# Computing the first key pair by eight plain products, and splitting the context on VectorE

## The reference, cut to what matters

```python
x = _rmsnorm(hidden_states, ln_weight)
h_q = (x @ w_q.T).reshape(b, lq, H, DH)
h_k = (key_value_states @ w_k.T).reshape(b, lk, H, DH)   # key_value_states is ctx_4096
h_v = (key_value_states @ w_v.T).reshape(b, lk, H, DH)
score = jnp.einsum('bqhd,bkhd->bhqk', h_q, h_k) + position_bias[None]
```

## Time and profile before

| | us |
|---|---|
| Median of 3 runs | 1058.89 |
| Lowest and highest run | 1058.1, 1059.1 |
| The profiled execution, its own time | 1058.91 |
| Its span, first to last instruction | 1056.8 |
| TensorE busy in the span | 1014.0 (96%) |
| VectorE, ScalarE, GpSimd busy | 730.2, 505.9, 481.7 |

### The profile page before, as it was taken

How to read it: one execution, slowest core, us unless ns; L and a number is a source line. 1 busy time by engine, 2 the same in 40 slices (tenths; PEclk the granted TensorE clock), 3 DMA queues, 4 the chain that set the end, 5 groups by cost and what they waited for, 6 DMA issues and landing times.

```text
span 1056.8 us, 17513 instructions
## 1 busy us (share of the span) xinstructions
PE 1014.0 (96%) x5850; PEld 887.6 (84%) x5850; DVE 730.2 (69%) x1316; ACT 505.9 (48%) x1226; POOL 481.7 (46%) x413
## 2 busy tenths in 40 slices
PE   8599999989999999999999999999999999799995
PEld 8488788878999998989898989898999998578784
DVE  6968776647777777676767676767777777663615
ACT  6545444535455455454454554545545455344251
POOL 2645776436345354363553544535535443443204
PEclk9799999999999999999999999999999999899998
DMA  7433444431221221202112212021121230300011
GB/s 259 139 117 123 150 167 162 173 123 52 91 65 52 79 74 42 92 25 92 62 55 79 66 50 91 26 92 62 54 80 41 75 112 21 110 20 1 0 41 40
DMA packets 39140, 86.07 MB, mean 81 GB/s; under 512 B 5184, under 2 KB 9280, under 8 KB 39104
## 3 DMA queue, kind: packets, MB, share of 16 engines
q1 hardware_dynamic: 39104, 85.62, 24.0%
HBM read 66.73 MB, written 18.87 MB: 81 GB/s over the span
## 4 chain that ended last, share of the span: by engine, by line
PE 85%; DVE 7%; POOL 3%; ACT 2%; issue 2%; DMA 1%; DVEq 0%; SPq 0%; POOLq 0%; ACTq 0%
PE psum L1625 24%; PE psum L1627 24%; PE psum L1626 23%; PE psum L1631 8%; PE psum L1632 3%; PE psum L1781 3%; DMA raw<-in_dft 1%; DVE av_lo L1201 1%; POOL cx_lo L766 1%; DVE smx L1342 1%; DVE mix L1201 0%; POOL mix L606 0%; POOL stat L758 0%; POOL stat L756 0%; ACT smx L1011 0%
## 5 line engine op out<-in xcount | busy, mean ns | idle before, releaser
L606 POOL TENSOR_TENSOR mix<-kf,mix 128x512 fp32r<-128x512 f32 x64 | 113.9, 1780 | 141.6 <-ACT mix L822 141.6
L657 POOL TENSOR_TENSOR smx<-far,bias 128x512 f32<-128x512 f32 x64 | 83.3, 1301 | 178.2 <-DVE smx L1293 175.8
L1625 PE MATMUL psum<-wvq_lo,cx_hi 128*128 128x256 f32 x512 | 149.6, 292 | 2.1 <-DVE av_lo L1201 2.1
L1627 PE MATMUL psum<-wvq_hi,cx_hi 128*128 128x256 f32 x512 | 144.8, 283 | 0.0
L1626 PE MATMUL psum<-wvq_hi,cx_lo 128*128 128x256 f32 x512 | 144.6, 282 | 0.0
L1011 ACT ACTIVATE smx<-smx,nmax 128x128 f32<-128x128 f32 x256 | 99.8, 391 | 82.6 <-DVE nmax L1299 82.6
L822 ACT ACTIVATE av_hi<-psum 128x512 fp32r<-128x512 f32 x140 | 83.9, 599 | 105.2 <-PE psum L1632 67.0
L1625 PE MATMUL psum<-mix,av_hi 128*128 128x512 f32 x256 | 106.0, 414 | 1.0 <-issue 1.0
L1201 DVE TENSOR_TENSOR av_lo<-psum,av_hi 128x512 fp32r<-128x512 f32 x76 | 52.6, 692 | 77.3 <-ACT av_hi L822 77.3
L1625 PE MATMUL psum<-xn_lo,wvq_hi 128*128 128x512 f32 x272 | 106.0, 390 | 0.0
L1627 PE MATMUL psum<-xn_hi,wvq_hi 128*128 128x512 f32 x272 | 105.9, 389 | 0.0
(11 more groups left out here) (214 smaller groups left out, 2707.2 us busy)
## 6 DMA issues: line engine op xcount, KB each, us to landing
kf<-k_blocks SPq DMA_DIRECT2D x64, 256.0 KB, 2.6
raw<-in_wk SPq DMA_DIRECT2D x16, 512.0 KB, 3.6
k_blocks<-far SPq DMA_DIRECT2D x32, 256.0 KB, 2.2
raw<-in_wv SPq DMA_DIRECT2D x16, 512.0 KB, 4.9
raw<-in_wq SPq DMA_DIRECT2D x16, 512.0 KB, 3.8
raw<-in_wo SPq DMA_DIRECT2D x16, 512.0 KB, 3.4
raw<-in_ffn SPq DMA_DIRECT2D x10, 512.0 KB, 3.6
k_blocks<-smx SPq DMA_DIRECT2D x16, 256.0 KB, 2.0
```

Of the source, the lines that this page charges most:

```text
L606: g.tensor_tensor(dst_lo, src, dst_hi, ALU.subtract).then_inc(s_lo, 1)
L657: nc.gpsimd.tensor_tensor(bm, far[:, HB * hf:HB * hf + HB, :], g_, ALU.add).then_inc(s_bm_ready, 1)
L1625: mm(out, lhs(0), rhs(1), start=first, stop=False)
L1627: return mm(out, lhs(0), rhs(0), start=False, stop=last)
```

## The change

Pair 0 of the keys is computed without sums: four blocks of `hp` (head) and `hf` (half of the context rows), each with four chunks of depth, are eight block products, 48 matmuls (`k0_block`). Their weights are the two parts of the whole weight piece, kept in `kf` (`k0_weights`). ScalarE copies the four banks to the staging tiles (`k0_copy`). The seven-product scheme begins with pair 1, and all the side work that was hung on pair *p* hangs on pair *p* + 1; the sums of weights that GpSimd made for pair 0 fall away.

The four context low parts move from GpSimd to VectorE (`ctx_lo`), into VectorE's list before and after `t_sums(0)`. The list there becomes `ctx_lo(0)`, `ctx_lo(1)`, `t_sums(0)`, `ctx_lo(2)`, `ctx_lo(3)`, `t_low(0)`, the low part of pair 0's weights, `t_sums(1)`, `square_lo(1, 0..3)`, `t_low(1)`, the low parts of pair 1's summed weights, `top`.

Ahead of the attention, the first value product now precedes the first query projection, and the second value product writes bank 1 in place of bank 3. Some semaphores are merged (mask with norm weights, and two pairs that count steps of one engine).

The diff, cut to its core (most lines left out replace `p` by `q = p - 1` in a count or by `p + 1` in a condition):

```diff
@@ block.sync @@
+            def k_consumed(p):
+                if p == 0:
+                    sp.wait_ge(s_k0_lo, 1)
+                else:
+                    sp.wait_ge(s_ks_plo, 3 * p)
+                    sp.wait_ge(s_ks_vlo, 4 * p)
...
             def load_block(g, j):
                 if is_first(g):
+                    sp.wait_ge(s_k0_mm, 4)
                     sp.wait_ge(s_kst[j], 16)
...
-                for i in (C22, C11, C21, C12):
+                for i in (C22, C11, C21, C12) if p else range(4):
                     store_block(p, i)
@@ block.gpsimd @@
-            ctx_lo(0)
-            ctx_lo(1)
-            ctx_lo(2)
-            ctx_lo(3)
-            k_sums(0)
-            k_weights_lo(0, A11, 1)
-            k_weights_lo(0, A12, 2)
-            k_last_sum(0)
-            k_weights_lo(0, A22, 3)
-            for p in range(PAIRS):
+            k_sums(1)
+            k_weights_lo(1, A11)
+            k_weights_lo(1, A12)
+            k_last_sum(1)
+            k_weights_lo(1, A22)
+            for p in range(1, PAIRS):
@@ block.scalar @@
+            def k0_hi():
+                pc = k_piece(0)
+                act.wait_ge(s_landed[pc % SLOTS], 16 * (pc // SLOTS + 1))
+                copy_hi(k0_weights(0), raw[:, pc % SLOTS]).then_inc(s_k0_hi, 1)
+
+            def k0_copy(i):
+                act.wait_ge(s_k0_mm, i + 1)
+                if i == C22:
+                    act.wait_ge(s_tt_lo, 8)
+                a.activation(staged[i], banks[i], ACT.Copy).then_inc(s_c[i], 1)
...
-            ctx_hi(0)
-            ctx_hi(1)
+            for n in range(CTX_PIECES):
+                ctx_hi(n)
             t_hi(0)
-            ctx_hi(2)
-            ctx_hi(3)
-            t_hi(1)
-            for block in range(BLOCKS):
-                k_weights_hi(0, block)
-            for tile in range(HB):
-                lag0(tile)
-                mirror(tile)
+            k0_hi()
             for j in range(4):
                 square(1, j)
-            for p in range(PAIRS):
+            t_hi(1)
+            k0_copy(C11)
+            for block in (A11, S2, S3, S1):
+                k_weights_hi(1, block)
+            k0_copy(C21)
+            for block in (A12, A22, S4):
+                k_weights_hi(1, block)
+            lag0(0)
+            mirror(0)
+            lag0(1)
+            mirror(1)
+            k0_copy(C12)
+            lag0(2)
+            mirror(2)
+            lag0(3)
+            mirror(3)
+            k0_copy(C22)
+            for p in range(1, PAIRS):
                 k_pair_act(p)
...
+            hi_of(s_v_mm, s_v_hi, 1, value_dst(0, 0), psV[:, :].rearrange("p (b n) -> p b n", b=2))
             hi_of(s_q_mm, s_q_hi, 1, qk[0][:, 0], psQ[:, :])
             k_hi(0, 0, 0)
-            hi_of(s_v_mm, s_v_hi, 1, value_dst(0, 0), psV[:, :].rearrange("p (b n) -> p b n", b=2))
-            hi_of(s_v_mm, s_v_hi, 2, value_dst(0, 1), psV[:, :].rearrange("p (b n) -> p b n", b=2))
+            hi_of(s_v_mm, s_v_hi, 2, value_dst(0, 1), banks[1].rearrange("p (b n) -> p b n", b=2))
@@ block.vector @@
+            def ctx_lo(n):
+                c = CTX_ORDER[n]
+                dve.wait_ge(s_cx_hi, n + 1)
+                lo_part(cx[1][:, c], raw[:, (DFT_PIECES + n) % SLOTS], cx[0][:, c]).then_inc(s_cx_lo, 1)
+
+            ctx_lo(0)
+            ctx_lo(1)
             t_sums(0)
+            ctx_lo(2)
+            ctx_lo(3)
             t_low(0)
+            dve.wait_ge(s_k0_hi, 1)
+            lo_part(k0_weights(1), raw[:, k_piece(0) % SLOTS], k0_weights(0)).then_inc(s_k0_lo, 1)
             t_sums(1)
+            for j in range(4):
+                square_lo(1, j)
             t_low(1)
             for block in (S2, S3, S1, S4):
-                k_weights_lo(0, block)
-            top(0)
-            top(1)
-            top(2)
-            top(3)
-            for j in range(4):
-                square_lo(1, j)
-            for p in range(PAIRS):
+                k_weights_lo(1, block)
+            for tile in range(HB):
+                top(tile)
+            for p in range(1, PAIRS):
                 k_pair_dve(p)
@@ block.tensor @@
+            def k0_block(i):
+                if i == 0:
+                    pe.wait_ge(s_k0_lo, 1)
+                    pe.wait_ge(s_cx_lo, CTX_PIECES)
+                pe.wait_ge(s_sq_lo, 4 + i + 1)
+                hp, hf = i % 2, i // 2
+                for c in range(DC):
+                    n = hp * HALF + c * P
+                    last = mm3(banks[i][:, :], lambda k: k0_weights(k)[:, n:n + P],
+                               lambda k: cx[k][:, c, hf * HALF:(hf + 1) * HALF], c == 0, c == DC - 1)
+                last.then_inc(s_k0_mm, 1)
...
-                if p == 0 and block == A11:
-                    pe.wait_ge(s_cx_lo, CTX_PIECES)
+                if q == 0 and block == S2:
                     pe.wait_ge(s_tt_lo, 8)
-                if p == 0 and block in (A11, S2, S3, S1):
-                    pe.wait_ge(s_sq_lo, 4 + block + 1)
+                if q == 0 and block < 4:
+                    pe.wait_ge(s_c[block], 1)
...
                 if isinstance(n, int) and n == 0:
                     pe.wait_ge(s_xt_lo, B)
-                    pe.wait_ge(s_tu4, PAIRS)
+                    pe.wait_ge(s_c[C12], PAIRS)
...
-                    if due(m):
+                    if isinstance(m, int) and m < 3:
+                        pe.wait_ge(*((s_c[C21], PAIRS), (s_tu4, PAIRS - 1), (s_v_lo, 1))[m])
+                    else:
                         pe.wait_ge(s_v_lo, m)
-                    else:
-                        pe.wait_ge(s_c[C12], PAIRS)
+                bank = banks[1] if isinstance(m, int) and m == 1 else psV
...
             dft(1)
-            for p in range(PAIRS):
+            for i in range(4):
+                k0_block(i)
+            for p in range(1, PAIRS):
                 k_pair_pe(p)
-                if p == 0:
+                if p == 1:
                     count_general(0)
...
-            project(0, 0, 0)
             values(0, 0, 0, 0)
             values(0, 0, 0, 1)
+            project(0, 0, 0)
             values(1, 0, 2, 0)
             values(1, 0, 2, 1)
             scores(0)
```

More of the change, by code:

```diff
@@ L121, in build, with product_bank @@
         psO = [banks[1], psT]
-        def product_bank(p, block):
-            return banks[(BLOCKS * p + block) % 4]
+        def product_bank(q, block):
+            return banks[(BLOCKS * q + block) % 4]
         def parts(first):
@@ L195, in build @@
         s_lag0 = sem("lag0")
-        s_others = sem("others")
+        s_k0_hi = sem("k0_hi")
+        s_k0_lo = sem("k0_lo")
+        s_k0_mm = sem("k0_mm")
         s_nonzero = sem("nonzero")
@@ L330, in whole, with k0_weights @@
             return raw[:, slot]
+        def k0_weights(i):
+            return kf[:, i * PIECE:(i + 1) * PIECE]
         def k_half(p, block):
@@ L689, in k_pair_pool @@
                     k_sums(p + 1)
-                    k_weights_lo(p + 1, A11, 1)
-                if p in (2, 5):
[L692 to L700, removed]
+                    k_weights_lo(p + 1, A11)
+                if p in (3, 6):
+                    factors(p // 3 - 1)
+                if p in (6, 8, 10, 12):
+                    weighted_row(p - 6)
+                    weighted_row(p - 5)
+                if p + 1 < PAIRS:
+                    k_weights_lo(p + 1, A12)
+                    k_last_sum(p + 1)
+                    k_weights_lo(p + 1, A22)
+                if p in (2, 5):
                     shifted_rows(p // 3)
@@ L784, in w_power @@
             def w_power(tile):
-                pool.wait_ge(s_w_stats_b, tile + 1)
+                pool.wait_ge(s_w_stats, 2 * tile + 2)
                 nc.gpsimd.tensor_scalar(stat[:, tile, 4:5], mv[:, tile, 0:1], -1.0, None, ALU.mult
@@ L905, in k_weights_hi @@
                 else:
-                    act.wait_ge(s_s_sum, 4 * p + {S3: 1, S1: 2, S2: 3, S4: 4}[block])
-                if p == 0:
+                    act.wait_ge(s_s_sum, 4 * q + {S3: 1, S1: 2, S2: 3, S4: 4}[block])
+                if q == 0:
                     act.wait_ge(s_dft_mm, 4)
                 else:
-                    act.wait_ge(s_kp_mm, BLOCKS * (p - 1) + block + 1)
+                    act.wait_ge(s_kp_mm, BLOCKS * (q - 1) + block + 1)
                 copy_hi(k_weights(0, block), k_half(p, block)).then_inc(s_ks_hi, 1)
             def x_copy(p):
-                act.wait_ge(s_kp_mm, BLOCKS * p + 1)
-                if due(p):
-                    act.wait_ge(s_c[C11], p)
-                a.activation(xcopy, product_bank(p, A11), ACT.Copy).then_inc(s_xc, 1)
+                q = p - 1
+                act.wait_ge(s_kp_mm, BLOCKS * q + 1)
+                act.wait_ge(s_c[C11], p)
+                a.activation(xcopy, product_bank(q, A11), ACT.Copy).then_inc(s_xc, 1)
             def k_pair_act(p):
@@ L1424, in k_pair_dve @@
-                if p == 2:
+                dve.wait_ge(s_kp_mm, BLOCKS * q + A12 + 1)
```

(11 more changed lines are left out.)

194 lines of the change are left out of this document (89 added, 105 removed).

## The result

The changed kernel takes 1042.29 us (median of four runs, 1042.08 to 1043.07) against 1058.64 for the kernel before (the three runs of the table above and a fourth, 1058.1 to 1059.1). The ratio is 0.9847, with a 95% interval of 0.983 to 0.9864: 16.35 us less, where 16.2 was forecast. The profiled execution took 1042.18, with a span of 1040.4, so the spans differ by 16.4.

A forecast was written before the change was run, and what follows sets the result against it. TensorE, busy for 96% of the span, bounds the kernel, with a 13.0 us stop set by VectorE's list. 1058.9 - 13.8 (pair 0) - 2.4 (attention's entry) = 1042.7 us, range 1040.5 to 1046.0.

The forecast's parts named there:

- The stop: TensorE ahead of pair 0: 13.0 us, ended by VectorE's `square_lo`; VectorE's list is the chain; shrinks to 0.3.
- The 0.3 us charged: Ahead of pair 0's first product: TensorE still waits 0.3 us for `square_lo(1, 0)`, between 0 and 1.5.
- The rule named in the prediction: VectorE instructions with two SBUF inputs and GpSimd instructions reading SBUF exclude each other; by it alone, 1043.9 us.
- rival (c): VectorE ahead of pair 0: `t_sums(1)` is held throughout by GpSimd, 1.2 us more, 1043.9 us; chance 0.10.
- the charge of 0.3 for the count: Pair 1's counting product: its input is there at 57.0 to 57.9, TensorE at 57.7; 0.3 us charged.
- The first part: Pair 0 and what moves behind it: old 25.3 us, new 0.3 + 10.9 + 0.3 = 11.5, gain 13.8.
- The entry: Start of the attention: value products' two waits for bank 3, 1.50 and 0.63 us, fall away; gain 2.4 at most.
- signs of being wrong: Stop over 2 us before the first block, clock 0.50, stop over 1 at `S1` or count, or transposes awaiting probabilities.
- With so short a stop I expect no fall: TensorE's granted clock ahead of pair 0: stays at 1.00 behind a stop of 0.3 us.
- Rival (b): Pair 0's weights are late: TensorE stands 2.4 us, plus 2.5 if the clock falls; 1047.6 us, chance 0.07.
- Rival (d): VectorE stays at the slow pace, both sets of sums at 7 us each; 1052.9 us, chance 0.03.
- rival (e): Attention loop settles in an order where each of 64 units stops; at 0.3 us each 1061.9, slower; chance 0.05.

The follow-up runs named there:

- The three list edits: On the kernel before, one at a time: context's low parts to VectorE, 1054.3 us; squares forward, 1054.71; second value product into bank 1, 1055.72.

## Why the prediction was right, point by point

**The stop was VectorE's list.** Shown from both sides: moving the context's steps or the squares alone shortens it, putting either back into the changed kernel brings 2.2 or 5.1 us of it back. Of the 13.0 us none is left. The 0.3 us charged was not paid, since VectorE was 2.0 earlier than forecast (`square_lo(1, 0)` at 34.49, not 36.5). The term that was mis-sized is `t_sums(1)`: 3.7 us by the forecast, 34.49 - 31.95 = 2.5 in the trace, since GpSimd's first step began 0.2 later than forecast and VectorE's sums over 0.8 earlier. The remaining 0.8 are small: `ctx_lo` follows at 1.14 in place of 1.23 each. The rate that the forecast took from the earlier trace rows for four subtractions with GpSimd idle (2.49) is in part from beside a GpSimd step, which began at 29.81; the changed kernel has the same 2.49 with GpSimd idle throughout, so the term stands.

**GpSimd's pace.** The rule named in the prediction (the Trainium skill, SBUF — State Buffer, section Who interferes with whom) made rival (c). In the changed kernel it did not come true, since the two sets of steps passed each other; with VectorE 2 us later it did, 1.11 to 1.23 a sum. The runs agree with the rule. Rival (c)'s 1043.9 itself, which would be a stop of 1.5 us, was not produced by any run.

**Eight products.** 10.88 us, forecast 10.9. That the eighth is needed was not argued in the prediction; the run with seven shows it.

**Behind it.** The last copy ended at 50.05 (forecast 50.5), and pair 1's `S1` began at 51.77, so the cover was 1.7 us (1.8). `u2` was at 50.68, the counting product's input at 56.54, 5.86 later (5.74 before, start to start); the charge of 0.3 for the count came out as 0.1. The first part gained 14.5 in place of 13.8, of which 0.5 are the two charges of 0.3 that fell to 0 and 0.1. The other 0.2 are no work of the change: the transform ended at 36.59 in place of 36.79, and over all the traces it ends anywhere from 36.37 to 37.22, so two executions can differ by that much there.

**The entry.** 2.3 of 2.4 forecast. The step behind it was only half right: the stops for the bank went, but the first softmax took back 0.41 at the transposes, waiting for the late bias, which the prediction had described and then charged nothing for. That wait is one of its own signs of being wrong, and it came true in small. Counted from the end of the keys, the key's low part came 2.9 us later (7.0 in place of 4.1), as forecast, but the mask `far` did not: it began after 7.0 us as before, so the two met at 210.4, and `far` took 1.80. The bias came 1.1 us later, not 2.5 to 3. Against that the second scores' stop shrank from 0.97 to 0.60, which the forecast had not counted.

**The clock.** "With so short a stop I expect no fall" was not put to the test, as there was no stop. The nearest runs are the one with seven products, where the clock stayed at 1.00 behind a stop of 1.78 us, and those with stops of 2.06 to 2.36 us, where it fell in the executions profiled. Rival (b)'s 2.5 us for a fallen clock, taken from the stop of 13 us, would have been about 1.75 for a stop of its length. Its condition did not come in: ScalarE rounded the first weight piece from 29.60 to 30.66, and VectorE took it at 30.82 without a wait. Rival (d), 1052.9, comes nearest to the run with the context's steps on GpSimd, which took 1045.97: the second set of sums is not held there, because GpSimd has done its four steps by 32.3 and begins its next one at 37.92.

**The loop's rhythm,** rival (e): the shift of 14.5 us at the end of the keys is 16.79 at the transposes of the third unit (252.50 to 235.71) and 16.81 at TensorE's last matmul (1044.14 to 1027.33), so the loop gave nothing back. Behind that matmul the end of the program took 0.4 us longer, which leaves the 16.4 of the spans.

**How near the sum came.** That 16.35 lies within 0.2 of the 16.2 forecast is partly luck: the first part gained 0.7 more than forecast, the entry 0.1 less, and 0.4 went at the end of the program, where nothing had been forecast.

## What to carry to other kernels

When an engine's list is the chain, count what the neighbour does to its steps before counting the steps: here four steps of 1.2 us each were added to the bound engine and its list got shorter. The three list edits nearly add up: 4.1, 3.7 and 3.0 us one at a time on the kernel before, 10.2 together. The eighth product, dearer by 1.4 us, brought nearly 6 more beside them, since it took TensorE off the chain of sums, copies and count, and with the stop the low clock went too. A stop of 2 us can cost some 1.75 us of clock behind it, so what ends such a stop can be worth more than its length.

## What the runs showed of the hardware beside this

A VectorE step with one SBUF operand can be held too: `far`, 128 by 1024 from uint8 to float32, took 1.80 us where GpSimd's 1.29 us step on the key had begun 0.04 earlier, and 0.69 where nothing of GpSimd's ran beside it. The section of the Trainium skill named above lists `tensor_scalar`, the operation that makes `far`, among those that can contend with GpSimd when their operands meet certain conditions. The pair of runs agrees.

After a stop of 1.78 us TensorE's granted clock stayed at 1.00. After stops of 2.06, 2.11, 2.17, 2.36 and 3.00 us it fell to 0.50, the lower level, and cost about 1.7 us each time in the executions profiled; after 5.04 us it cost 2.7. After 13.0 us it cost 2.5, so the price does not grow in proportion to the stop.
